# An LSTM scan with a modulated projection on one core: the filler matmuls of TensorE taken out

## The chip, the cores and the metric

The kernel runs on one core of a Trainium2 chip. The metric is the device time of one execution in microseconds, as the median of several runs. Beside it stands one execution recorded by the hardware profiler, from which all rows below are taken.

## The reference

The input x has 2 sequences of 1024 steps with 256 features, cond has one row of 256 per sequence. An LSTM with start state cond runs over x, and its output is added to x. Then a projection, whose input is scaled by cond and whose output is normalised, is added to that.

```python
def step(carry, xw_t):                       # xW = x @ Wx + b, for all steps
    prev_h, prev_c = carry
    a = xw_t + prev_h @ Wh
    i = sigmoid(a[:, :H]); f = sigmoid(a[:, H:2*H]); o = sigmoid(a[:, 2*H:3*H])
    g = tanh(a[:, 3*H:])
    next_c = f * prev_c + i * g
    next_h = o * tanh(next_c)
    return (next_h, next_c), next_h
x = x + lstm(x, h0=cond)                     # h0 = cond, c0 = 0
ys = cond / sqrt(256)
d = rsqrt((ys * ys) @ (w * w) + 1e-8)
x = x + ((x * ys[:, None, :]) @ w) * d[:, None, :]
```

All is fp32: B = 2 sequences, 1024 steps, H = D = 256, four gates.

## The kernel before

Everything lies with features on the partitions: 256 features are K = 2 halves (index j or k) of 128. The 1024 LSTM steps depend on each other and are done one after the other, in a hardware loop of 64 rounds (NBODY) with 16 steps each (BODY), written out as two sets (index st) of T = 8 steps. Set st has its PSUM tensors pA[st][j]; the steps of a set are numbered t = 0 to 7.

One step passes through four stations, and semaphores hand it on:

- TensorE, `rec` (line 179): h of the step times Wh, added in PSUM to what stands there. The output of a half has 4 chunks of 32 partitions, one matmul each (c). The moving operand is 128 columns of Wh (four gates of 32), or 64 where only two gates are done. Per step these are five calls of four matmuls: half k=0 of h into j=0 and, two gates only, into j=1; then, when the second half of h is there, k=1 into j=0 (`sums_ready[0]`), the other two gates of k=0 into j=1, and k=1 into j=1 (`sums_ready[1]`).
- VectorE: two transposes of 128x128 from PSUM to `turned` (line 276), one for each j; later four cell updates (line 281, each with a read of the accumulator) and two products o * tanh(c) (line 289), which write h of the next step into `hst` and raise `h_ready[j]`.
- ScalarE: a sigmoid for each j over all gates (line 151), and tanh of c for each j (line 155).

While set st is worked on, the other set's PSUM is filled with bias and x @ Wx by `fill` (lines 167 and 170). There are six such calls, (j, part) for j in 0, 1 and part in 0, 1, 2, of four matmuls each. They stand behind the `rec` calls of the steps t = 2 to 7, one per step; t = 0 and 1 have none.

The filler (line 160) is a matmul of `ones` (32 columns as the stationary operand) with 128 columns of Wh into the PSUM tensor pD. Nobody reads it. `PRODUCTS = 2` sets how many products follow the `rec` calls of each step: a `fill` counts as one, and fillers make up the rest. So t = 0 and 1 have two fillers, t = 2 to 7 one. Another 24 fillers stand in front of the loop, behind the first set's `fill` calls and a wait for `demod_added`.

TensorE works through its instructions in the order in which they are written. GpSimd (POOL) copies x for the next fills into `xr` and adds h to x, eight steps at a time. Ahead of the loop weights and x are loaded, the gate columns of g are doubled, and the four matmuls of line 187 sum for the normalisation. Behind the loop 16 matmuls of 512 columns (line 231) do the projection, VectorE adds (line 297), and eight DMAs write the output.

Of the kernel before, what the change touches and what calls it, by code (L numbers as in the profile page):

```python
# [4 lines left out]
P = 128  # L5
# [6 lines left out]
def build(nc, xT_in, condT_in, Wx, Wh, bT, w, outT):  # L12
# [3 lines left out]
    Q = P // G  # L16
# [6 lines left out]
    CELL = 16  # L23
    AT_G, AT_HALF, AT_C = 9, 10, 11
    HEAD = G // 2
    PRODUCTS = 2
    NOUT = 512
    NCH = SEQ // NOUT

# [1 line left out]
    with ctx:  # L31
        def sb(name, shape):
            return ctx.enter_context(nc.sbuf_tensor(name, shape, F32))
# [5 lines left out]
        wh_sb = sb("wh_sb", [P, K, G * D])  # L39
        bias_sb = sb("bias_sb", [P, G * D])  # L40
        ones = sb("ones", [P, Q])
# [18 lines left out]
        pD = ctx.enter_context(nc.psum_tensor("pD", [P, 512], F32))  # L60
# [23 lines left out]
        def chunk(of, c, j, lo=0, hi=G):  # L84
            return of.rearrange("p (g d) -> p g d", g=G)[:, lo:hi, j * P + c * Q:j * P + (c + 1) * Q]
# [8 lines left out]
        @block.sync  # L94
        def _(sp):
            sp.dma_start(wx_sb[:, :, :], Wx.rearrange("(k p) g -> p k g", p=P)).then_inc(wx_loaded, 16)
            for lo, hi in zip(XCUT, XCUT[1:]):
                for k in range(K):
                    sp.dma_start(xh[:, k, :, lo:hi], xT_in[k * P:(k + 1) * P, :, lo:hi]).then_inc(  # L99
                        x_loaded if lo else x_begun, 16)  # L100
            sp.dma_start(w_sb[:, :, :], w.rearrange("(k p) o -> p k o", p=P)).then_inc(w_loaded, 16)

            for n, (b, ch, o) in enumerate(UNITS):
                sp.wait_ge(result_ready, n + 1)
                sp.dma_start(outT[o * P:(o + 1) * P, b, ch * NOUT:(ch + 1) * NOUT], ores[:, n % 2, :]).then_inc(out_written[n % 2], 16)
            for n in range(2):
                sp.wait_ge(out_written[n], 16 * (len(UNITS) // 2))
# [48 lines left out]

        @block.tensor
        def _(pe):
            def filler():
                pe.matmul(pD[0:Q, 3 * P:4 * P], ones[:, :], wh_sb[:, 0, 0:P], start=True, stop=True)  # L160

            def fill(st, j, part):
                for c in range(G):
                    rows = slice(c * Q, (c + 1) * Q) if part == 0 else slice(c * Q, c * Q + ROWS)
                    into = pA[st][j][rows, 0:P].rearrange("p (g u) -> p g u", g=G)
                    if part == 0:
                        last = pe.matmul(into, ones[:, :], chunk(bias_sb[:, :], c, j),  # L167
                                         start=True, stop=False, skip_group_check=True)
                    else:
                        last = pe.matmul(into, xr[:, st, part - 1, :, :], chunk(wx_sb[:, part - 1, :], c, j),  # L170
                                         start=False, stop=False, skip_group_check=True)
                return last

            FILLS = [(j, part) for j in range(K) for part in range(1 + K)]

            def rec(st, t, j, k, lo=0, hi=G):
                M = B * (t + 1)
                for c in range(G):
                    last = pe.matmul(pA[st][j][c * Q:c * Q + M, lo * Q:hi * Q].rearrange("p (g u) -> p g u", u=Q),  # L179
                                     hst[:, st, k, Q * t:Q * t + M], chunk(wh_sb[:, k, :], c, j, lo, hi),  # L180
                                     start=False, stop=True, skip_group_check=True)
                return last

            pe.wait_ge(squares_ready, 1)
            for o in range(K):
                for k in range(K):
                    last = pe.matmul(pD[:, o * B:(o + 1) * B], wsq[:, k, o * P:(o + 1) * P], ysq[:, k, :],  # L187
                                     start=(k == 0), stop=(k == K - 1))
            last.then_inc(demod_summed, 1)

            pe.wait_ge(operands_ready, 4)
            pe.wait_ge(xr_ready, 1)
            for j, part in FILLS:
                last = fill(0, j, part)
            last.then_inc(filled, 1)
            pe.wait_ge(demod_added, 1)
            for _ in range(24):
                filler()

            with pe.Fori(0, NBODY) as it:  # L200
                for s in range(BODY):
                    st, t = divmod(s, T)

                    pe.wait_ge(h_ready[0], it * BODY + (s + 1))
                    rec(st, t, 0, 0)
                    rec(st, t, 1, 0, 0, HEAD)

                    pe.wait_ge(h_ready[1], it * BODY + (s + 1))
                    rec(st, t, 0, 1).then_inc(sums_ready[0], 1)
                    rec(st, t, 1, 0, HEAD, G)  # L210
                    rec(st, t, 1, 1).then_inc(sums_ready[1], 1)

                    work = 0
                    n = t - (T - len(FILLS))
                    if n >= 0:
                        work = 1
                        if n == 0:
                            pe.wait_ge(xr_ready, it * SETS + (st + 2))
                        last = fill(1 - st, *FILLS[n])
                        if n == len(FILLS) - 1:  # L220
                            last.then_inc(filled, 1)
                    for _ in range(PRODUCTS - work):
                        filler()

            pe.wait_ge(wmod_ready, B * K)
            pe.wait_ge(xh_ready, SETS * NBODY + 1)
            for n, (b, ch, o) in enumerate(UNITS):
                if n >= 2:
                    pe.wait_ge(result_ready, n - 1)
                for k in range(K):  # L230
                    last = pe.matmul(pO[n % 2][:, :], wmod[:, b, k, o * P:(o + 1) * P],  # L231
                                     xh[:, k, b, ch * NOUT:(ch + 1) * NOUT], start=(k == 0), stop=(k == K - 1))
                last.then_inc(layer_summed, 1)
# [93 lines left out]
```

## Time and profile before

| what | value |
|---|---|
| median of 3 runs | 2243.52 us (2242.71 to 2243.88) |
| the profiled execution, its own time | 2243.01 us |
| its span, first to last instruction | 2241.2 us |
| PE (TensorE matmul) busy | 1542.8 us, 69% |
| PEld (TensorE weight load) busy | 1253.7 us, 56% |
| DVE (VectorE) busy | 1404.2 us, 63% |
| ACT (ScalarE) busy | 855.0 us, 38% |
| POOL (GpSimd) busy | 116.3 us, 5% |

The span lies 1.8 us below the time of the same execution. In the profile PE is TensorE's matmul and PEld its weight load, which overlaps the matmuls. Each fp32 matmul of the code has two load records and two matmul records. The ends of matmuls are modelled, so the starts and the loads tell more of the pace than the busy time does. "Granted clock" is the share of TensorE's full speed that the chip allowed. The numbers x8, x40 and so on count records; a name such as `pA<-wh_sb,hst` is output and inputs.

### The profile page before, as it was taken

The numbers are of one execution on the slowest core, as the hardware profiler recorded it, in microseconds if no ns is written. First come the engines' busy times: TensorE is split into PE (matmuls) and PEld (weight loads), VectorE is DVE, ScalarE is ACT, GpSimd is POOL, SyncE is SP. The second block draws the span as 40 slices with busy tenths as digits, with TensorE's granted clock in tenths as the row PEclk, the third lists the DMA queues.
The fourth block names the chain that finished last, engine by engine and source line by source line (L and its number), as shares of the span: only waits on it lengthen the run. The fifth ranks groups of instructions, "written<-read, shape, count | busy, mean of one in ns | idle before, by whom it ended". The sixth has DMA issues, their size and how long they took to land.

```text
span 2241.2 us, 121713 instructions
## 1 busy us (share of the span) xinstructions
PE 1542.8 (69%) x49800; PEld 1253.7 (56%) x49800; DVE 1404.2 (63%) x12314; ACT 855.0 (38%) x4100; POOL 116.3 (5%) x648
## 2 busy tenths in 40 slices
PE   5666666666666666666666666666666666666666
PEld 4555555555555555555555555555555555555554
DVE  4666666666666666666666666666666666666665
ACT  2333333333333333333333333333333333333332
POOL 0000000000000000000000000000000000000000
PEclk9999999999999999999999999999999999999999
DMA  2000000000000000000000000000000000000000
GB/s 82 0 0 0 0 0 0 0 0 0 0 0 0 0 0 0 0 0 0 0 0 0 0 0 0 0 0 0 0 0 0 0 0 0 0 0 0 0 0 37
DMA packets 4428, 6.70 MB, mean 3 GB/s; under 512 B 1089, under 2 KB 2881, under 8 KB 4418
## 3 DMA queue, kind: packets, MB, share of 16 engines
q1 hardware_dynamic: 3872, 5.51, 0.7%
q10 hardware_dynamic: 546, 1.05, 0.1%
q8 instruction: 7, 0.11, 0.0%
q14 instruction: 3, 0.02, 0.0%
HBM read 4.46 MB, written 2.10 MB: 3 GB/s over the span
## 4 chain that ended last, share of the span: by engine, by line
DVE 46%; PE 37%; ACT 10%; issue 6%; DMA 0%; SPq 0%; POOLq 0%; POOL 0%
PE pA L179 36%; DVE turned L276 29%; DVE junk L281 11%; ACT gates L151 10%; DVE hst L289 5%; DVE gates L281 1%; PE pO L231 1%; DMA w_sb<-in_w_dram 0%; PE pD L160 0%; SPq L99 0%; PE pD L187 0%; PE pA L170 0%; PE pA L167 0%; DVE ores L297 0%; DVE wsq L256 0%
## 5 line engine op out<-in xcount | busy, mean ns | idle before, releaser
L179 PE MATMUL pA<-wh_sb,hst 128*2 128x128 f32 (+3 forms) x40960 | 1092.7, 252 | 676.7 <-DVE hst L289 676.7
L179 PEld LDWEIGHTS pA<-wh_sb,hst 128*2 128x2 f32 (+1 forms) x40960 | 793.5, 90 | 956.0 <-DVE hst L289 951.3
L276 DVE STREAM_TRANSPOSE turned<-pA 128x128 f32<-128x128 f32 x2048 | 650.2, 317 | 561.0 <-PE pA L179 548.5
L151 ACT ACTIVATE gates<-turned 128x8 f32<-128x8 f32 x2048 | 442.3, 216 | 1222.1 <-DVE turned L276 1106.1
L281 DVE CUSTOM_DVE_ANT_0 junk<-gates 128x4 f32<-128x4 f32 x4096 | 504.6, 161 | 76.5
L155 ACT ACTIVATE tanhc<-gates 128x2 f32<-128x2 f32 x2048 | 418.2, 204 | 128.2
L160 PE MATMUL pD<-wh_sb,ones 128*32 128x128 f32 x2608 | 452.5, 273 | 0.0
L289 DVE TENSOR_TENSOR hst<-tanhc,gates 128x2 f32<-128x2 f32 x2048 | 330.9, 162 | 172.1 <-ACT tanhc L155 172.1
L281 DVE DVE_READ_ACCUMULATOR2_ANT gates<- 128x1 f32 x4096 | 340.3, 83 | 0.0
L160 PEld LDWEIGHTS pD<-wh_sb,ones 128*32 128x32 f32 x2608 | 285.8, 110 | 1.0
L170 PE MATMUL pA<-wx_sb,xr 128*16 128x128 f32 x4128 | 207.9, 274 | 0.0
L129 POOL TENSOR_TENSOR xh<-xh,hst 128x14 f32 x256 | 56.9, 222 | 2083.0 <-DVE hst L289 2083.0
L170 PEld LDWEIGHTS pA<-wx_sb,xr 128*16 128x16 f32 x4128 | 117.2, 97 | 0.3
L167 PE MATMUL pA<-bias_sb,ones 128*32 128x128 f32 x2064 | 104.3, 274 | 0.0
L167 PEld LDWEIGHTS pA<-bias_sb,ones 128*32 128x32 f32 x2064 | 61.9, 110 | 0.1
L131 POOL TENSOR_TENSOR xh<-xh,hst 128x2 f32 x256 | 49.5, 193 | 0.0
L115 POOL COPY xr<-xh 128x32 f32 (+1 forms) x130 | 28.0, 216 | 23.6 <-PE pA L170 10.8
L231 PE MATMUL pO<-xh,wmod 128*128 128x512 f32 x32 | 14.0, 594 | 2.0 <-POOL xh L131 2.0
L187 PE MATMUL pD<-ysq,wsq 128*128 128x2 f32 x8 | 1.9, 355 | 16.0 <-DVE wsq L256 16.0
L297 DVE SCALAR_TENSOR_TENSOR ores<-pO,demod,xh 128x512 f32<-128x512 f32 x8 | 6.0, 751 | 9.8 <-PE pO L231 9.8
L231 PEld LDWEIGHTS pO<-xh,wmod 128*128 128x128 f32 x32 | 6.0, 190 | 9.4 <-issue 9.2
L187 PEld LDWEIGHTS pD<-ysq,wsq 128*128 128x128 f32 x8 | 1.8, 328 | 16.0 <-DVE wsq L256 16.0
(24 smaller groups left out, 9.6 us busy)
## 6 DMA issues: line engine op xcount, KB each, us to landing
outT_dram<-ores SPq DMA_DIRECT2D x8, 256.0 KB, 2.5
xh<-in_xT_dram SPq DMA_DIRECT2D x6, 320.0 KB, 7.9
wx_sb<-in_Wx_dram SPq DMA_DIRECT2D x1, 1024.0 KB, 5.2
wh_sb<-in_Wh_dram ACTq DMA_DIRECT2D x1, 1024.0 KB, 7.6
w_sb<-in_w_dram SPq DMA_DIRECT2D x1, 256.0 KB, 8.4
xh<-in_xT_dram SPq DMA_DIRECT2D x2, 64.0 KB, 7.5
condT<-in_condT_dram ACTq DMA_DIRECT2D x1, 2.0 KB, 5.4
bias_sb<-in_bT_dram ACTq DMA_DIRECT2D x1, 4.0 KB
```

The lines of the kernel that those rows point to most:

```text
L129: pool.tensor_tensor(most, most, slots(st, j, 1, T).rearrange("p t b -> p b t"), ALU.add)
L131: done = pool.tensor_tensor(last, last, slots(1 - st, j, 0, 1).rearrange("p t b -> p b t"), ALU.add)
L151: act.activation(gates[:, j, :, 0:3 * G:3].rearrange("p b g -> p g b"), turned[:, j, :, B * t:B * (t + 1)], ACT.Sigmoid).then_inc(gates_re ...
L155: act.activation(tanhc[:, j, :], gates[:, j, :, AT_C], ACT.Tanh, scale=2.0).then_inc(tanh_ready[j], 1)
L160: pe.matmul(pD[0:Q, 3 * P:4 * P], ones[:, :], wh_sb[:, 0, 0:P], start=True, stop=True)
L167: last = pe.matmul(into, ones[:, :], chunk(bias_sb[:, :], c, j), start=True, stop=False, skip_group_check=True)
L170: last = pe.matmul(into, xr[:, st, part - 1, :, :], chunk(wx_sb[:, part - 1, :], c, j), start=False, stop=False, skip_group_check=True)
L179: last = pe.matmul(pA[st][j][c * Q:c * Q + M, lo * Q:hi * Q].rearrange("p (g u) -> p g u", u=Q), hst[:, st, k, Q * t:Q * t + M], chunk(wh_ ...
L231: last = pe.matmul(pO[n % 2][:, :], wmod[:, b, k, o * P:(o + 1) * P], xh[:, k, b, ch * NOUT:(ch + 1) * NOUT], start=(k == 0), stop=(k == K ...
L276: dve.transpose(turned[:, j, :, :].rearrange("p g r -> p (g r)"), pA[st][j][:, 0:P]).then_inc(turned_ready[j], 1)
L281: cell = dve.tensor_tensor_reduce(out=junk[:, j, b, :], in0=gates[:, j, b, 0:4:3].unsqueeze(2).broadcast_to([P, 2, 2]), in1=gates[:, j, b, ...
L289: dve.tensor_tensor(hcols((s + 1) % BODY, j), tanhc[:, j, :], gates[:, j, :, 6], ALU.mult).then_inc(h_ready[j], 1)
```

## The change

The definition of the filler, its two calls and the constant that counts them are taken out. The calls of `rec` and `fill`, their order and all waits stay.

```diff
-    PRODUCTS = 2
...
-            def filler():
-                pe.matmul(pD[0:Q, 3 * P:4 * P], ones[:, :], wh_sb[:, 0, 0:P], start=True, stop=True)
-
...
             last.then_inc(filled, 1)
             pe.wait_ge(demod_added, 1)
-            for _ in range(24):
-                filler()
...
                     rec(st, t, 1, 1).then_inc(sums_ready[1], 1)

-                    work = 0
                     n = t - (T - len(FILLS))
                     if n >= 0:
-                        work = 1
                         if n == 0:
                             pe.wait_ge(xr_ready, it * SETS + (st + 2))
                         last = fill(1 - st, *FILLS[n])
                         if n == len(FILLS) - 1:
                             last.then_inc(filled, 1)
-                    for _ in range(PRODUCTS - work):
-                        filler()
```

## Rows read from the trace of the kernel before

**Rows 1.** The page: span, busy time, chain by engine, the group of transposes.

```profile
span 2241.2 us, 121713 instructions
PE 1542.8 (69%) x49800; PEld 1253.7 (56%) x49800; DVE 1404.2 (63%) x12314; ACT 855.0 (38%) x4100; POOL 116.3 (5%) x648
...
DVE 46%; PE 37%; ACT 10%; issue 6%; DMA 0%; SPq 0%; POOLq 0%; POOL 0%
...
L276 DVE STREAM_TRANSPOSE turned<-pA 128x128 f32<-128x128 f32 x2048 | 650.2, 317 | 561.0 <-PE pA L179 548.5
```

**Rows 2.** Timeline of one step: start us, duration us, engine, line, operation, tiles, records.

```profile
1001.78 0.79 PEld L179 LDWEIGHTS pA<-wh_sb,hst 128*16 128x16 f32 x40 [0.93 <-DVE hst L289]
1002.56 0.23 PEld L170 LDWEIGHTS pA<-wx_sb,xr 128*16 128x16 f32 x8
1002.59 0.65 DVE L276 STREAM_TRANSPOSE turned<-pA 128x128 f32<-128x128 f32 x2 [0.54 <-PE pA L179]
1002.67 0.40 PE L170 MATMUL pA<-wx_sb,xr 128*16 128x128 f32 x8
1002.78 0.22 PEld L160 LDWEIGHTS pD<-wh_sb,ones 128*32 128x32 f32 x2
1002.89 0.38 PE L160 MATMUL pD<-wh_sb,ones 128*32 128x128 f32 x2
...
1003.93 0.44 PEld L179 LDWEIGHTS pA<-wh_sb,hst 128*2 128x2 f32 x24 [0.93 <-DVE hst L289]
```

**Rows 3.** Busy time over the whole loop: stretch, busy us, granted clock, DMA.

```profile
25.70:2222.40 2196.70, 1519.15 (x49668) 1238.64 (x49665) 1393.52 (x12288) 852.06 (x4096) 113.45 (x635) 1.00 0.00 0
```

**Rows 4.** Timeline from the first matmul to the first step.

```profile
15.99 1.78 PEld L187 LDWEIGHTS pD<-ysq,wsq 128*128 128x128 f32 x8 [15.99 <-DVE wsq L256]
...
18.01 0.81 PEld L170 LDWEIGHTS pA<-wx_sb,xr 128*16 128x16 f32 x16
18.86 0.41 PEld L167 LDWEIGHTS pA<-bias_sb,ones 128*32 128x32 f32 x8
19.11 0.21 DVE L268 COPY hst<-condT 128x2 f32<-128x2 f32 x2
19.29 0.81 PEld L170 LDWEIGHTS pA<-wx_sb,xr 128*16 128x16 f32 x16
20.14 5.67 PEld L160 LDWEIGHTS pD<-wh_sb,ones 128*32 128x32 f32 x48
25.70 0.96 PEld L179 LDWEIGHTS pA<-wh_sb,hst 128*2 128x2 f32 x40
26.68 0.44 PEld L160 LDWEIGHTS pD<-wh_sb,ones 128*32 128x32 f32 x4
```

**Rows 5.** Line 170's records, ns min/median/max, before the loop and in it.

```profile
L170 PEld LDWEIGHTS pA<-wx_sb,xr x32: 146/146/146, 18.0 to 19.9; 128*16 128x16 f32 x32
L170 PE MATMUL pA<-wx_sb,xr x32: 417/418/418, 18.2 to 20.2; 128*16 128x128 f32 x32
...
L170 PEld LDWEIGHTS pA<-wx_sb,xr x72: 97/97/97, 1000.4 to 1034.9; 128*16 128x16 f32 x72
L170 PE MATMUL pA<-wx_sb,xr x72: 272/273/273, 1000.5 to 1035.0; 128*16 128x128 f32 x72
```

**Rows 6.** Filler loads of line 160, from 20.1 to 20.8 and from 21.0 us.

```profile
L160 PEld LDWEIGHTS pD<-wh_sb,ones x4: 173/173/173, 20.1 to 20.8; 128*32 128x32 f32 x4
...
L160 PEld LDWEIGHTS pD<-wh_sb,ones x44: 110/110/118, 21.0 to 25.7; 128*32 128x32 f32 x44
```

**Rows 7.** A stretch near the end: busy us, granted clock, DMA.

```profile
2239.60:2239.80 0.20, 0.00 (x0) 0.00 (x0) 0.00 (x0) 0.00 (x0) 0.00 (x0) 0.65 1.00 389
```

**Rows 8.** Timeline of TensorE at the end of the loop and of the kernel.

```profile
2221.13 0.38 PE L160 MATMUL pD<-wh_sb,ones 128*32 128x128 f32 x2
2223.54 0.67 PE L231 MATMUL pO<-xh,wmod 128*128 128x512 f32 x1 [2.02 <-POOL xh L131]
...
2235.63 1.88 PE L231 MATMUL pO<-xh,wmod 128*128 128x512 f32 x4
```

## The prediction

> **What bounds the kernel now.** I read four views in this order. The page comes first: no engine is busy for the whole span, TensorE (PE) for 69% and VectorE for 63%, and the chain of waits is DVE 46%, PE 37%, ACT 10% [rows 1]. So the kernel is bound by a latency chain that hands over from engine to engine, and an engine's idle time in it costs nothing by itself.
>
> Then the timeline of one step in the middle of the loop [rows 2]. A step begins when DVE has written h for j=0 and PE starts at 1001.78. DVE's first transpose starts at 1002.59, 0.81 us later; the two transposes take 0.65, the sigmoids, cell updates and tanh follow, and the next step's PE work starts at 1003.93, so a step is 2.15 us. All 1024 of them stand between 25.70 and about 2222.4, or 2196.7/1024 = 2.145 us each [rows 3]. Behind its 40 records of `rec` (20 matmuls in the code, two records each) PE does 8 of `fill` and 2 of the filler, and its weight loads then stop for 0.93 us until h comes. In the two steps of eight that have no `fill` there are 4 filler records instead, 0.44 us of loads [rows 4]; the idle time before the next h is the same.
>
> Third, the start [rows 4]. PE's last `fill` record before the loop belongs to a load run from 19.29; the loads of the 24 fillers begin at 20.14 and the loop's first at 25.70. DVE had copied h0 at 19.11 to 19.32. So nothing but the fillers holds the first step from 20.14 on.
>
> Fourth, TensorE's clock. The granted clock reads 1.00 over the whole loop [rows 3], which is the level of 2.4 GHz. It also reads 1.00 at the start, but there the durations contradict it: the same 128-column `fill` record takes 418 ns there and 273 ns in the loop, and its load 146 ns against 97 ns [rows 5]. I go by the durations: PE began at 1.2 GHz. Filler loads show the rise: 173 ns up to 20.8, 110 ns from about 21.0 [rows 6]. PE had then worked without a rest from 15.99, some 4.9 us. At the other end the granted clock drops to 0.5 near 2239.66 (0.65 over the slice 2239.6 to 2239.8) [rows 7]; PE's last matmuls, a group from 2235.63 of 1.88 us [rows 8], ended at 2237.51, only about 2.15 us earlier.
>
> **The change part by part.**
>
> 1. The 24 fillers in front: 48 records, 5.56 us (20.14 to 25.70) on the path. Their removal lets step 0 start at 20.14. What was hidden behind them is in time: h0 is there at 19.32 [rows 4], and POOL's wait concerns only a later set. But the clock rose at about 20.9, so the first 0.8 us of step 0 would still run at half pace, which loses 0.4. Net **-5.2 us**. Bounds: -5.56 if nothing is slow, -4.6 if all of step 0 is.
>
> 2. The fillers in the steps, on the path: nothing. They end at 1003.27 (0.38 us after 1002.89) where PE next waits until 1003.93 [rows 2]; nobody reads what they write, and their PSUM tensor is not the one that DVE transposes. I cost the removal at **0**, hidden by that wait. DVE's transposes, beside which they run, take 317 ns each in every step [rows 1]; in the step shown they start with `fill` beside them, 1002.59 against 1002.56 [rows 2]. No step shows a transpose without matmuls beside it, so a small gain or loss is not excluded; the mean step of the loop (2.145) and the step shown (2.15) agree to 0.005 us although a quarter of the steps has fillers only, and I bound the effect by that, 5 us over 1024 steps.
>
> 3. The fillers in the steps, for the clock: this decides. PE's rest in its loads grows from 0.93 to 0.93 + 0.22 = 1.15 us in six steps of eight and 0.93 + 0.44 = 1.37 us in two. Whether the clock stands this is not in the trace. First the price of one step at 1.2 GHz. Loads of `fill` come each (18.86 - 18.01)/16 = 53 ns at the start [rows 4] against (1002.78 - 1002.56)/8 = 27.5 ns in the loop [rows 2], so +26 ns for a 128-column record. The 40 records of `rec` fill 1001.78 to 1002.67 = 0.89; less 24 x 27.5 ns this leaves 14 ns for each of the 16 of 64 columns, and I take +13 ns for those. In front of the first transpose stand 16 records of 128 and 8 of 64 columns: 16 x 26 + 8 x 13 = 520 ns. The last record's duration grows by 418 - 273 = 145 ns. The second transpose needs 8 of 64 and 8 of 128 more: 8 x 13 + 8 x 26 = 310 ns, and now PE needs 0.33 for them while the first transpose covers about 0.32, so all 310 lie open. Sum 0.52 + 0.145 + 0.31 = **0.98 us a step**. Bounds: 0.77 if 64-column records don't slow at all (they may be paced by issue), 1.18 if they slow by 26 ns too. Other engines' terms don't change.
>
> How often? What the rows bound: rests of 0.93 us in every step held at 2.4 GHz over 2197 us; one rest of 2.02 us at 2221.5 to 2223.5 held too [rows 8]; one of 2.15 at the end didn't. Both last ones stand alone, with dense work ahead of them, while in the changed loop a rest comes in every step, and rests of 1.37 come two in a row. So 0 steps and all 1024 are both open. I take the clock to fall around the pair of steps without `fill`, where the rests are longest, and to come back in the six with it: low for 2 of 8 steps, 256 steps x 0.98 = **+251 us**. Sum against the profiled execution, whose time is 2243.0 beside a span of 2241.2 [rows 1]: 2243.0 - 5.2 + 0 + 251 = 2488.8; the median of the runs is 0.5 above it: **2489 us**. Low in a sixteenth of the steps it would be 64 x 0.98 = 63, 2301; in half of them 502, 2740. This is the case's own range.
>
> The Trainium skill speaks against this. "TensorE: Matmul & The Clock Gate", section "Why this matters for your kernels", warns of idle gaps of over about 3 us between bursts; by that rule the clock would hold here, and the sum would be that of the first rival. The trace agrees with it for the gaps of 0.93 and 2.02 us and not at the end, where 2.15 us were enough. The same page's section on a second failure mode (PSUM-queue cycling) tells of a kernel whose frequent short idles made the clock go to and fro; by that the sum is the one above.
>
> **The rivals.**
>
> A. The clock holds: 2243.5 - 5.2 = **2238.3 us**, faster by 0.23%. For it: 2.02 us held once, and the new rests are 1.15 and 1.37. Against: they recur in every step, and the clock needed 4.9 us of unbroken work to rise, which suggests that more than the longest rest counts. This is the case of the other sign; it decides from the point where not even the pair of steps without `fill` brings the clock down. About five steps at 1.2 GHz in the whole loop eat its gain (5.2/0.98).
>
> B. The clock falls and stays: after a fall the loop never again offers PE what the start did, work without a rest (at 1.2 GHz a step still has about 1 us of rest). Then 2243.5 - 5.2 + 1024 x 0.98 = **3242 us**; with the bounds of the price 3027 to 3447. For it: the only rise in the trace stands behind unbroken work. Against: at the low level the same records take PE longer, so that it rests less, and the one rise says nothing of how little would do.
>
> C. The change doesn't do what it says (PE busy by other work, or the removed records replaced): the diff removes every caller of the filler and adds nothing, so I give it no chance of its own.
>
> **How the numbers follow.** Forecast (falls and comes back) 0.41, A 0.32, B 0.27. A measurement here tells a difference of about 0.2%, 4.5 us. Faster by more than that: most of A, 0.28, since its gain of 5.2 is barely over the bound. Within it: 0.04, A with less gained at the start or a few slow steps. Slower: 0.68, the forecast and B. The range starts at 2236 (A with the full 5.56, and 2 us of item 2) and ends at 3260, which holds B at its taken price and leaves out its upper part and the extremes, under 2 in 10. It is this wide because three cases each hold over a quarter. The likeliest one's own range is 2301 to 2740.
>
> **What would show it.** Filler rows gone; the first `rec` load at about 20.1. With the clock held: 418 ns records only ahead of the loop, granted clock 1.00, step 2.15. With my forecast: granted clock between 0.5 and 1.0 in every slice (about 0.85), `rec` records at both 273 and about 418 ns, steps of 2.15 and 3.13 side by side, the slow ones about those with h of t = 0 and 1. With B: 0.5 throughout and every step 3.1. I am wrong in the price if a slow step isn't 2.9 to 3.3 us, and wrong in the cause if the time changes while durations stay at 273 ns.

## The result and the profile after

| | median | runs |
|---|---|---|
| before | 2243.39 us | 4, 2242.71 to 2243.88 |
| changed | 2320.51 us | 4, 2309.70 to 2334.85 |

The changed kernel is slower: ratio 1.0349, with a 95% interval of 1.0297 to 1.040. Its own runs spread by 1.1%, those of before by 0.05%. The profiled execution took 2311.57 us.

The page of the changed kernel, span and busy times first, then the groups that answer to those of before:

```profile
span 2309.8 us, 116497 instructions
PE 1365.1 (59%) x47192; PEld 1024.2 (44%) x47192; DVE 1395.6 (60%) x12314; ACT 849.7 (37%) x4100; POOL 116.0 (5%) x648
...
DVE 44%; PE 40%; ACT 10%; issue 6%; DMA 0%; SPq 0%; POOLq 0%; POOL 0%
...
L266 DVE STREAM_TRANSPOSE turned<-pA 128x128 f32<-128x128 f32 x2048 | 649.5, 317 | 628.6 <-PE pA L175 616.4
```

Against [rows 1] there are 2608 fewer records on PE and as many fewer on PEld, the same counts on DVE, ACT and POOL, and the same 317 ns for a transpose. What grew is DVE's wait for PE in front of the transposes, and PE's share of the chain, from 37% to 40%. So time came into TensorE's part of the step and into no other.

The list of cores (span, mean granted clock), where before it had a mean of 1.000:

```profile
core 0: 2309.8 us, clock 0.947
```

Stretches of the changed kernel (busy us of PE, PEld, DVE, ACT, POOL; then granted clock, DMA share, GB/s):

```profile
20.95:130.00 109.05, 62.14 (x2333) 47.52 (x2326) 69.19 (x611) 42.37 (x204) 5.38 (x31) 1.00 0.00 1
130.20:133.50 3.30, 2.69 (x68) 1.91 (x62) 1.32 (x13) 0.76 (x4) 0.00 (x0) 0.50 0.00 0
...
645.60:652.30 6.70, 5.03 (x112) 3.32 (x115) 2.68 (x25) 1.59 (x9) 0.00 (x0) 0.50 0.00 0
652.40:703.50 51.10, 29.15 (x1095) 22.26 (x1091) 32.48 (x288) 19.97 (x96) 2.65 (x15) 1.00 0.00 0
703.60:706.90 3.30, 2.70 (x68) 1.98 (x60) 1.30 (x13) 0.76 (x4) 0.00 (x0) 0.50 0.00 0
```

The clock holds at first for over 100 us, then falls to half (0.50, the level of 1.2 GHz) for a short time, holds again, falls again. "A fall" is one such stretch from here on. With a mean of 0.947 and only the levels 1.0 and 0.5, the time at the low one is 2 x (1 - 0.947) x 2309.8 = 245 us. Steps at full clock and at the low clock, from the timeline of the changed kernel. The step t has 2(t + 1) columns of h in its last name, so 128*2 is t = 0, 128*4 is t = 1 and so on:

```profile
641.30 0.79 PEld L175 LDWEIGHTS pA<-wh_sb,hst 128*16 128x16 f32 x40 [1.14 <-DVE hst L279]
642.08 0.23 PEld L166 LDWEIGHTS pA<-wx_sb,xr 128*16 128x16 f32 x8
643.45 0.77 PEld L175 LDWEIGHTS pA<-wh_sb,hst 128*2 128x2 f32 x40 [1.14 <-DVE hst L279]
645.58 1.39 PEld L175 LDWEIGHTS pA<-wh_sb,hst 128*4 128x4 f32 x40 [1.37 <-DVE hst L279]
648.52 1.40 PEld L175 LDWEIGHTS pA<-wh_sb,hst 128*6 128x6 f32 x40 [1.55 <-DVE hst L279]
...
651.46 1.19 PEld L175 LDWEIGHTS pA<-wh_sb,hst 128*8 128x8 f32 x40 [1.08 <-DVE hst L279]
```

The steps from 641.30 and 643.45 take 2.15 and 2.13 us, as before [rows 2]; the rests in front of a load run are 1.14 us, and 1.37 behind a step without `fill`, as worked out. The steps from 645.58 and 648.52 (t = 1 and 2) lie wholly at the low clock and take 2.94 us each. The next fall, at 703.6, lies later in its eight steps, at t = 3 and 4:

```profile
701.23 0.77 PEld L175 LDWEIGHTS pA<-wh_sb,hst 128*6 128x6 f32 x40 [1.37 <-DVE hst L279]
703.37 1.25 PEld L175 LDWEIGHTS pA<-wh_sb,hst 128*8 128x8 f32 x40 [1.13 <-DVE hst L279]
706.14 1.17 PEld L175 LDWEIGHTS pA<-wh_sb,hst 128*10 128x10 f32 x40 [1.08 <-DVE hst L279]
```

Counted over the trace of all 1024 steps, 49 of the 128 sets of eight have one fall and the others none. 22 falls begin late in t = 0 and reach into t = 3; the other 27 begin in t = 2 or 3 and end in t = 4 at the latest. From 630 us on they come in a regular rhythm, two falls every 71.7 us. So the clock falls at or shortly behind the pair without `fill`, and in most sets not at all. The loop is 72 us longer than before.

DVE's two transposes in the step from 648.52:

```profile
649.84 0.32 DVE L266 STREAM_TRANSPOSE turned<-pA 128x128 f32<-128x128 f32 x1 [1.02 <-PE pA L175]
650.48 0.32 DVE L266 STREAM_TRANSPOSE turned<-pA 128x128 f32<-128x128 f32 x1 [0.32 <-PE pA L175]
```

The first starts 1.32 us after PE's first load instead of 0.81, and the second no longer follows at once but waits another 0.32. And the median matmul record takes 417 ns, as at the start [rows 5]; line 175 between 646 and 649.5:

```profile
L175 PE MATMUL pA<-wh_sb,hst x60: 311/417/421, 645.8 to 649.4; 128*4 128x128 f32 x20, 128*4 128x64 f32 x16, 128*6 128x128 f32 x16, 128*6 128x64 f32 x8
```

At the start the loop now begins 5.6 us earlier (20.09 instead of 25.70):

```profile
19.24 0.81 PEld L166 LDWEIGHTS pA<-wx_sb,xr 128*16 128x16 f32 x16
20.09 1.27 PEld L175 LDWEIGHTS pA<-wh_sb,hst 128*2 128x2 f32 x40
22.75 0.77 PEld L175 LDWEIGHTS pA<-wh_sb,hst 128*4 128x4 f32 x40 [1.38 <-DVE hst L279]
```

Its first step takes 2.66 us, 0.5 more than a fast one: its load run takes 1.27 us instead of 0.77, so it starts at the low pace. So 5.1 of the 5.6 us are gained.

### The profile page after: what moved, and what is told of

It is laid out like the page before. It is cut to its first block, busy times and chain, and to the rows that moved or that the text cites. A ratio compares the mean times of both kernels' runs of the same rounds, so it can differ in the third digit from the quotient of the medians.

```text
span 2309.8 us, 116497 instructions
## 1 busy us (share of the span) xinstructions
PE 1365.1 (59%) x47192; PEld 1024.2 (44%) x47192; DVE 1395.6 (60%) x12314; ACT 849.7 (37%) x4100; POOL 116.0 (5%) x648
## 4 chain that ended last, share of the span: by engine, by line
DVE 44%; PE 40%; ACT 10%; issue 6%; DMA 0%; SPq 0%; POOLq 0%; POOL 0%
PE pA L175 39%; DVE turned L266 28%; DVE junk L271 11%; ACT gates L150 10%; DVE hst L279 5%; DVE gates L271 1%; PE pO L221 1%; DMA w_sb<-in_w_dram 0%; SPq L98 0%; PE pD L183 0%; PE pA L166 0%; PE pA L163 0%; DVE ores L287 0%; DVE wsq L246 0%; SPq L95 0%
## 5 line engine op out<-in xcount | busy, mean ns | idle before, releaser
L175 PE MATMUL pA<-wh_sb,hst 128*2 128x128 f32 (+3 forms) x40960 | 1167.2, 262 | 922.8 <-DVE hst L279 922.8
L175 PEld LDWEIGHTS pA<-wh_sb,hst 128*2 128x2 f32 (+1 forms) x40960 | 832.3, 93 | 1250.3 <-DVE hst L279 1224.2
L266 DVE STREAM_TRANSPOSE turned<-pA 128x128 f32<-128x128 f32 x2048 | 649.5, 317 | 628.6 <-PE pA L175 616.4
L166 PE MATMUL pA<-wx_sb,xr 128*16 128x128 f32 x4128 | 214.2, 281 | 0.0
L163 PE MATMUL pA<-bias_sb,ones 128*32 128x128 f32 x2064 | 110.3, 287 | 0.0
```

The costliest lines, as they stand in the source:

```text
L266: dve.transpose(turned[:, j, :, :].rearrange("p g r -> p (g r)"), pA[st][j][:, 0:P]).then_inc(turned_ready[j], 1)
```

## The experiments

All times are medians; each ratio is to runs of the kernel before on the same chip. "Bare" steps are those without `fill`, t = 0 and 1 of each eight. "The loss" is what the changed kernel takes more than the one before, 77 us.

### Which of the two removals does it

Only the 24 fillers out:

```diff
-            for _ in range(24):
-                filler()
```

> Only the 24 fillers in front of the loop are out; the fillers in the steps stay. Theory (the clock falls because of what the steps of the loop have TensorE do; the 24 are only a delay): the clock holds at 1.00 through the loop and the time is 5 us under before, 2238.2 (2237.5 to 2239). Rival (the 24 set the clock up and without them the loop starts low and stays unstable): part of the loop is at 0.5, time above 2243.

Measured: 2241.43 us, ratio 0.9986 (0.9976 to 0.9995), 3.5 us under the 2244.88 of before.

```profile
core 0: 2237.6 us, clock 0.999
```

The loop (25 to 2217 us) shows a granted clock of 1.00 throughout:

```profile
25.00:2217.00 2192.00, 1515.96 (x49561) 1236.43 (x49552) 1390.51 (x12264) 850.07 (x4088) 112.72 (x635) 1.00 0.00 0
```

The 24 are a delay in front of the loop, and not needed for its clock. Slightly less was gained than expected, 3.5 us instead of 5. The mean of 0.999 leaves about 4 us at the low clock, most of it behind the last step. There PE rests for 2.02 us until POOL is done, and the clock falls as the projection begins:

```profile
2218.21 4.08 PE L229 MATMUL pO<-xh,wmod 128*128 128x512 f32 x5 [2.02 <-POOL xh L131]
...
2218.70:2221.90 3.20, 3.20 (x5) 1.35 (x4) 0.15 (x1) 0.00 (x0) 0.00 (x0) 0.50 0.00 0
```

The kernel before has the same steps and the same rest of 2.02 us there [rows 8], and its clock held there.

Only the fillers in the steps out, the 24 kept:

```diff
-                    for _ in range(PRODUCTS - work):
-                        filler()
```

> The 24 fillers stay, the fillers in the steps are out. Theory (the steps alone do it): falls as in the changed kernel, mean clock 0.93 to 0.95, and the time of the changed kernel plus about 5 us, 2315 to 2340. Rival (start): clock 1.00 throughout, 2243.

Measured: 2309.89 us (2301.29 to 2317.57), ratio 1.0277 (1.0257 to 1.0297).

```profile
core 0: 2315.8 us, clock 0.947
```

The loop starts at full clock, and the clock falls nonetheless, first at about 68 us:

```profile
68.30:71.40 3.10, 2.50 (x60) 1.75 (x54) 1.30 (x13) 0.76 (x4) 0.00 (x0) 0.50 0.00 0
```

So of the two removals, that of the fillers in the steps makes the loss. The median was expected 5 us above the changed kernel's, at 2315 or more, and lies below that; 5 us are within the spread of these runs.

The changed kernel itself, once more:

> The changed kernel again, as the yardstick on this chip and for its own spread: 2300 to 2340, mean clock 0.93 to 0.95.

Measured: 2325.56 us (2319.68 to 2337.43), ratio 1.0365 (1.0326 to 1.0404).

```profile
core 0: 2327.5 us, clock 0.934
```

### Which steps need the fillers

Two in each bare step, none elsewhere, no 24:

```diff
-                    for _ in range(PRODUCTS - work):
+                    for _ in range(0 if work else 2):
                         filler()
```

> The changed kernel with two fillers put back in each of the two steps of eight that have no fill, and none elsewhere. Theory (the pair of steps without fill, where TensorE does least, brings the clock down): clock 1.00, time 2238 as with every filler but the 24. Rival (all steps count alike, only the total of work matters): 0.88 us of filler loads per 8 steps against 2.2 in before, so still falls, though rarer: 2250 to 2300.

Measured: 2240.50 us, ratio 0.998 (0.9971 to 0.999). The stretch from 25 us to the end of the work:

```profile
25.00:2236.00 2211.00, 1378.25 (x48072) 1084.44 (x48072) 1396.81 (x12278) 850.33 (x4090) 113.39 (x639) 1.00 0.00 1
```

One in each filled step, none in the bare ones, no 24:

```diff
-                    for _ in range(PRODUCTS - work):
+                    for _ in range(1 if work else 0):
                         filler()
```

> The changed kernel with one filler put back in each of the six steps that have fill, none in the two without. It adds 1.32 us of filler loads per 8 steps, more than the run before, but leaves the bare pair as it is. Theory (the bare pair): falls nearly as in the changed kernel, 2280 to 2340, mean clock under 0.97. Rival (the total of work): fewer falls than with fillers in the pair alone, time nearer 2238 than that run's.

Measured: 2245.90 us, ratio 1.0004 (0.9994 to 1.0013). Two stretches at full clock, each with the short fall behind it:

```profile
25.00:436.80 411.80, 264.81 (x9127) 211.14 (x9119) 260.96 (x2304) 159.61 (x768) 21.33 (x120) 1.00 0.00 0
437.00:440.20 3.20, 2.98 (x66) 2.16 (x58) 1.26 (x12) 0.77 (x4) 0.00 (x0) 0.50 0.00 0
440.40:849.80 409.40, 263.11 (x9061) 209.64 (x9050) 259.55 (x2292) 158.70 (x764) 21.33 (x120) 1.00 0.00 0
850.00:853.20 3.20, 2.98 (x66) 2.19 (x58) 1.26 (x12) 0.76 (x4) 0.00 (x0) 0.50 0.00 0
```

Falls are rare, once in over 400 us. My expectation missed: the bare pair was left as it was, and yet nearly all the loss is gone. What its neighbours do counts too. The five falls in the loop come 413 us apart, one in every 24 sets, each at the same place of its set (4.7 us behind the set's start). Yet all 128 sets have the same matmuls in the same order. So the order alone doesn't say whether a given set falls; how the steps lie in time counts as well, and no run varied that by itself. But these six fillers per eight steps do less than the four of the run above, which left no fall.

One in each bare step:

```diff
-                    for _ in range(PRODUCTS - work):
+                    for _ in range(0 if work else 1):
                         filler()
```

> The changed kernel with one filler in each of the two bare steps of eight: 0.44 us of filler loads per 8 steps, half of the run with two there, a third of the run with one in each filled step; every step then has the same load (8 records of fill or 2 of filler, 0.22 us) and the same rest of 1.15 us. Theory (the bare pair decides, and falls need the dip in it): clock 1.00 or nearly, 2238 to 2243. Rival (the total of work decides, little matter where): with less filler than either earlier run, more falls than with one filler in each filled step (mean clock under 0.99), 2255 to 2300.

Measured: 2240.03 us, ratio 0.9979 (0.9965 to 0.9993).

```profile
25.00:2219.00 2194.00, 1308.82 (x47533) 1022.09 (x47534) 1390.88 (x12268) 850.50 (x4089) 114.10 (x639) 1.00 0.00 0
```

No fall in the loop. A third of the filler work of the run with one in each filled step does more when it stands in the bare steps: the total of work alone is refuted, the place counts.

### The same work, dealt out differently

From here on no filler is left, unless the diff shows one. Bare steps apart, the six `fill` calls behind t = 1, 2, 3, 5, 6, 7:

```diff
+            FILL_AT = (1, 2, 3, 5, 6, 7)
...
-                    n = t - (T - len(FILLS))
-                    if n >= 0:
+                    if t in FILL_AT:
+                        n = FILL_AT.index(t)
```

> The changed kernel with its six fill calls behind steps t = 1, 2, 3, 5, 6, 7, so that the two bare steps (0 and 4) stand apart; no filler, no added work. Theory (two bare steps in a row bring the clock down): fewer falls than in the changed kernel, mean clock 0.97 or more, 2240 to 2285. Rival (total of work): as the changed kernel, 0.93 to 0.95 and 2305 to 2335. Second rival (the longest single rest, still 1.37 us): as the changed kernel too.

Measured: 2258.80 us, ratio 1.0061 (1.0047 to 1.0075).

```profile
core 0: 2256.8 us, clock 0.986
```

The same matmuls and the same longest rest of 1.37 us, and four fifths of the loss gone. Both rivals named there fall.

The 24 fill matmuls dealt out three to a step:

```diff
-            def fill(st, j, part):
-                for c in range(G):
+            def fill(st, j, part, chunks=range(G)):
+                for c in chunks:
...
-                    n = t - (T - len(FILLS))
-                    if n >= 0:
-                        if n == 0:
-                            pe.wait_ge(xr_ready, it * SETS + (st + 2))
-                        last = fill(1 - st, *FILLS[n])
-                        if n == len(FILLS) - 1:
-                            last.then_inc(filled, 1)
+                    if t == 0:
+                        pe.wait_ge(xr_ready, it * SETS + (st + 2))
+                    for n in range(3 * t, 3 * t + 3):
+                        last = fill(1 - st, *FILLS[n // G], (n % G,))
+                    if t == T - 1:
+                        last.then_inc(filled, 1)
```

> The changed kernel with its 24 fill matmuls dealt out three to a step (0.165 us of loads in each of the eight steps); no filler, no added work, every rest about 1.20 us. Theory (the dip decides): clock 1.00, 2238, the version that beats both kernels. Rival (total of work): mean clock 0.93 to 0.95 and 2305 to 2335, as the changed kernel.

Measured: 2240.32 us, ratio 0.998 (0.9966 to 0.9994). Over the loop, and behind it:

```profile
25.00:2217.00 2192.00, 1312.06 (x47012) 1024.61 (x47012) 1390.34 (x12262) 850.01 (x4087) 113.61 (x635) 1.00 0.00 0
2218.00:2224.00 6.00, 5.05 (x6) 2.18 (x7) 0.75 (x1) 0.00 (x0) 0.70 (x4) 0.50 0.00 0
```

With exactly the changed kernel's matmuls the clock holds through the loop. This version and the two with fillers in the bare steps alone beat both kernels; they are 4.2 to 4.5 us under before, and this one has no filler. Its one fall before the end lies behind the last step, where PE waits for POOL.

The same stretch of full clock in three versions with the same matmuls, first the changed kernel, then the bare steps apart, then three to a step:

```profile
25.00:110.00 85.00, 49.11 (x1840) 37.67 (x1832) 53.84 (x472) 32.66 (x157) 4.43 (x25) 1.00 0.00 1
25.00:110.00 85.00, 49.06 (x1840) 37.81 (x1840) 53.73 (x473) 32.65 (x157) 4.44 (x25) 1.00 0.01 1
25.00:110.00 85.00, 51.16 (x1840) 40.11 (x1840) 53.72 (x474) 32.65 (x157) 4.45 (x25) 1.00 0.01 1
```

PE is busy for the same time in the first two, so there the order alone took most of the loss away. The even version is busy for 2 us more in these 85, so it has that on its side too. But busy time in total doesn't decide either: with one filler in each filled step PE is busy for 0.643 of its first long stretch (264.81 of 411.8 us) and the clock falls, with one in each bare step for 0.597 (1308.82 of 2194) and it holds.

All the work in three steps, two calls each behind t = 5, 6, 7:

```diff
-                    n = t - (T - len(FILLS))
-                    if n >= 0:
-                        if n == 0:
+                    if t >= 5:
+                        if t == 5:
                             pe.wait_ge(xr_ready, it * SETS + (st + 2))
-                        last = fill(1 - st, *FILLS[n])
-                        if n == len(FILLS) - 1:
+                        for n in (2 * (t - 5), 2 * (t - 5) + 1):
+                            last = fill(1 - st, *FILLS[n])
+                        if t == T - 1:
                             last.then_inc(filled, 1)
```

> The changed kernel with its six fill calls two by two behind steps t = 5, 6, 7, and five bare steps in a row; the same work in all. Theory (what the least-worked stretch of steps holds): more falls than in the changed kernel, mean clock 0.80 to 0.92, 2350 to 2550. Rival (total of work): 0.93 to 0.95, 2305 to 2335. A slow step keeps its price: 0.30 us of time for each us at the low clock.

Measured: 2452.69 us, ratio 1.0917 (1.0883 to 1.0951).

```profile
core 0: 2456.9 us, clock 0.845
```

So the same matmuls give 2240, 2259, 2320 or 2453 us when they are dealt out otherwise; the longer the row of bare steps (none, one, two, five), the longer the clock is low. The price per microsecond at the low clock stays: this profiled run took 2458.71, less (2243.9 - 4.4) for a loop without falls, which is 219 us for 2 x 0.155 x 2456.9 = 762 us, 0.29. The changed kernel: 2311.6 - 2239.0 = 73 for 245, 0.30.

### Amount of work, or length of a rest

A matmul of 8 columns in each bare step, in the middle of its rest:

```diff
+                    if t < 2:
+                        pe.wait_ge(turned_ready[1], it * BODY + (s + 1))
+                        pe.matmul(pD[0:Q, 3 * P:3 * P + 8], ones[:, :], wh_sb[:, 0, 0:8], start=True, stop=True)
```

> The changed kernel with a matmul of 8 columns in each of the two bare steps, behind a wait for the second transpose, so that it falls into the middle of the rest: the rest of 1.37 us becomes two of about 0.7, and TensorE's work grows by next to nothing. Theory (the amount of work in the bare pair counts, not the length of a rest): falls as in the changed kernel, mean clock 0.93 to 0.96, 2295 to 2335. Rival (the longest rest without any matmul counts): clock 1.00, 2238.

Measured: 2265.05 us (2258.08 to 2284.71), ratio 1.0104 (1.0057 to 1.0151); the profiled run was the slowest of them:

```profile
core 0: 2282.9 us, clock 0.966
```

The same matmul without the wait, at once behind `rec`:

```diff
+                    if t < 2:
+                        pe.matmul(pD[0:Q, 3 * P:3 * P + 8], ones[:, :], wh_sb[:, 0, 0:8], start=True, stop=True)
```

> As the run with the matmul of 8 columns in the middle of the bare steps' rests (2265.1, 2258.1 to 2284.7), but issued at once behind rec, without the wait: the same work, and the rest of about 1.3 us in one piece. Theory (the amount of work counts): as that run, 2255 to 2290, mean clock 0.96 to 0.98. Rival (cutting the rest in two did it): as the changed kernel, 0.93 to 0.95 and over 2300.

Measured: 2317.19 us (2302.07 to 2336.53), ratio 1.0353 (1.0279 to 1.0428).

```profile
core 0: 2300.3 us, clock 0.954
```

At once it does nothing that could be told from the 2325.56 of the changed kernel on the same chip; in the middle of the rest it takes away most of the loss. The theory that I gave first missed in both: it isn't the amount of work alone. For the second run the rival came, 2317 and a clock of 0.954; for the first it had promised a clock of 1.00, and falls are left. How the two lie on PE (first the one in the middle, then the one at once):

```profile
1005.92 1.06 PE L175 MATMUL pA<-wh_sb,hst 128*2 128x128 f32 x40 [0.86 <-DVE hst L282]
1007.42 0.23 PE L209 MATMUL pD<-wh_sb,ones 128*32 128x8 f32 x2 [0.44 <-DVE turned L269]
```

```profile
1000.46 1.06 PE L175 MATMUL pA<-wh_sb,hst 128*4 128x128 f32 x40 [1.06 <-DVE hst L281]
1001.34 0.20 PE L208 MATMUL pD<-wh_sb,ones 128*32 128x8 f32 x2
```

At once, its 0.20 us lie almost wholly beside the last `rec` records, so PE is busy hardly longer; by itself it keeps PE busy for 0.23 us more. It cuts the rest in two and it adds busy time, and these two runs don't tell which of them helps.

The fill calls themselves moved into the rest, behind the second transpose:

```diff
                     if n >= 0:
+                        pe.wait_ge(turned_ready[1], it * BODY + (s + 1))
```

> The changed kernel with the fill call of each of the six filled steps behind a wait for the second transpose, so that the rest of 1.15 us is cut in two of about 0.7 and 0.4; the two bare steps keep their rest of 1.37 us, and the work is the same. If the longest rest decides, or the amount of work alone, it falls as the changed kernel, 2300 to 2340, mean clock 0.93 to 0.95. If the cutting up of rests counts everywhere (as the pair of runs with a matmul of 8 columns suggests, 2265.1 in the middle against 2317.2 at once), fewer falls, 2250 to 2295, clock over 0.955.

Measured: 2258.31 us (2258.22 to 2269.75), ratio 1.0065 (1.0049 to 1.0082).

```profile
1000.90 0.13 PEld L166 LDWEIGHTS pA<-wx_sb,xr 128*16 128x16 f32 x8 [0.72 <-DVE turned L267]
1001.54 0.77 PEld L175 LDWEIGHTS pA<-wh_sb,hst 128*2 128x2 f32 x40 [0.51 <-DVE hst L280]
1003.68 0.77 PEld L175 LDWEIGHTS pA<-wh_sb,hst 128*4 128x4 f32 x40 [1.37 <-DVE hst L280]
```

The filled steps' rest is now 0.72 and 0.51, the bare ones' 1.37 as ever; the same matmuls in the same order, and four fifths of the loss are gone. So neither the longest rest nor the count of matmuls decides alone. Here too PE is busy longer, 1469.3 us against 1365.1, as the fill no longer runs beside `rec`, so this run doesn't part the cut in the rest from the added busy time either.

## Why the prediction was right and wrong

**The start** (part 1): -5.2 us forecast; the trace shows 5.6 gained and 0.5 given back in the first step. Four versions without the 24 keep their clock through the loop: three come out 4.2 to 4.5 us under before, and the one with only the 24 taken out 3.5.

**The fillers as work** (part 2): right. Transposes stay at 317 ns and a fast step at 2.13 to 2.15 us, so taking the filler out of the steps costs and gains nothing while the clock holds.

**The price of a slow step** (part 3): 0.98 us forecast, 2.94 - 2.145 = 0.80 measured, near the lower bound. The second transpose's 0.31 came as worked out (0.32). The first transpose's term was too large: 0.52 + 0.145 = 0.665 forecast, 1.32 - 0.81 = 0.51 measured. The prices of the records were right: four records of 128 columns start 213 ns behind the four before them instead of 109, which is 26 a record, and four of 64 columns 107 instead of 56, which is 13. But from the first record's start to that of the last four in front of the transpose it is 0.834 us instead of 0.469, only 0.365 more. The forecast counted the spacing of these last four (4 x 26 = 104 ns) beside their longer duration, and the first four cost 55 ns of spacing instead of 104. Per microsecond at the low clock this matters little, 0.98/3.13 = 0.31 against 0.30 over the whole run.

**How often** (part 3) is the step that failed: "low for 2 of 8 steps", in every set of eight. The mechanism was the forecast one: falls near the pair without `fill`, returns, steps of both kinds side by side. But the share was chosen between 0 and 1024 steps from nothing that the trace could size. The forecast is 128 sets with 2 x 0.98 = 1.96 us each, 251 us. Measured are 49 sets with a fall, at 1.47 us each, 72 us; less the 5 us of the start these are nearly the 68 by which the profiled run is slower. In other terms, 245 us at the low clock are 83 slow steps of 2.94 us instead of 256. The places differ a little too: the slow steps were forecast at t = 0 and 1, and they are t = 1 to 4. Why 49 sets fall and 79 don't stays open. The time of 2320.5 lies inside the stated range, and inside the case's own range, near its lower end of 2301; the forecast of 2489 was off by 169 us, and that the measured time is inside owes more to the width of the range than to the estimate.

**The rivals.** A (the clock holds) was wrong for this order of the work, and right for an even one: the run with three fill matmuls a step has 2240.3, close to A's 2238.3. What decides between the two is how the same work is dealt out, which I had not seen as a choice. Its argument that a rest of 2.02 us had held is weak as well: with only the 24 taken out, the same code had a fall right behind the same rest. B (falls and stays) is refuted by every profile: the clock came back each time. Its reason, that the loop never offers unbroken work, was no obstacle: the clock was back in steps with rests of 1.08 and 1.15 us.

**The idle gaps.** The Trainium skill's page "TensorE: Matmul & The Clock Gate", in "Why this matters for your kernels", warns only of gaps over some 3 us. The trace of the changed kernel doesn't agree: its rests at full clock are 1.14 to 1.37 us, and the clock fell. The Trainium skill's other account on that page, in "A second HAM failure mode: psum-queue depth-cycling", tells of a kernel with frequent short idles whose clock goes to and fro. The trace agrees with it: 49 falls and as many returns in the loop.

## What to carry to other kernels

When TensorE works in a chain with rests of about 1 us, its clock is part of the kernel's schedule: look at the granted clock by stretch before and after taking away or moving any TensorE work, even work off the path. Before adding fillers, deal out the real off-path work evenly over the steps; here this did with no filler what 2.2 us of filler loads per eight steps had done. Putting it into the rests helped as well; the two together were not tried. And warm-up work in front of a loop is plain delay when the work already there brings the clock up.

## What was not expected of the hardware

- The same matmuls gave mean clocks of 0.998, 0.986, 0.947 and 0.845, depending on how they were dealt out over the steps.
- Short work in the middle of a rest (0.23 us of PE time) counted for much more than the same matmul placed beside other work: 2265 against 2317 us.
- The clock's return is easy: in each loop it came back from 0.5 with the loop's broken work, within some microseconds: the stretches of falls shown for the changed kernel are of 3.3 and 6.7 us, and the longest fall of any profile here, with five bare steps in a row, is of 13.7.
- With the bare pair left and the filled steps fuller, one fall came in over 400 us of loop. A kernel with falls also spreads more between executions (2309.7 to 2334.9) than one without (2238.7 to 2241.1). Identical sets of eight steps fall or hold at a regular distance, 413 us in that run; on what this distance depends was not tried, nor were the cut in a rest and the added busy time told apart.
